# Weight chunks reloaded as two half chunks, with a semaphore and a key for each half

## The reference

```python
# block 1: gated causal convolution, D_MODEL 2048, D_INNER 4096, 4 taps
xi, gate = split(layernorm(x) @ w_in.T)
xc = depthwise_causal_conv(xi, conv_w) + conv_b
x  = x + (silu(xc) * D * silu(gate)) @ w_out.T
# block 2: 8 experts (I_MOE 1024), top 2 of them weighted, and a shared FFN (I_SH 4096)
t = layernorm(x)
combine = normalised top-2 of softmax(t @ w_gate)
routed  = sum_e combine[:, e] * ((silu(t @ G_e) * (t @ U_e)) @ w_down_e)
shared  = (silu(t @ G_s) * (t @ U_s)) @ w_sh_down
x = x + routed + shared
```

## Time and profile before

| | us |
|---|---|
| median of 2 runs | 7186.25 |
| those runs | 7082.07 and 7290.44 |
| the profiled execution, time | 6710.59 |
| its span, slowest core (0) | 6709.0 |
| its spans, all cores | 6646.2 to 6709.0 |

### The profile page before, as it was taken

How to read it: one execution, slowest core, us unless ns; L and a number is a source line. 1 busy time by engine, 2 the same in 40 slices (tenths; PEclk the granted TensorE clock), 3 DMA queues, 4 the chain that set the end, 5 groups by cost and what they waited for, 6 DMA issues and landing times.

```text
span 6709.0 us, 69985 instructions; the slowest of 8 cores (6646.2 to 6709.0 us)
## 1 busy us (share of the span) xinstructions
PE 5761.2 (86%) x26243; PEld 2537.3 (38%) x26768; DVE 1529.4 (23%) x3001; ACT 984.1 (15%) x1469; POOL 1.3 (0%) x10
## 2 busy tenths in 40 slices
PE   4777899999699877776776798999999898999998
PEld 2333344433344333332332343444444343444443
DVE  3333233322222222222111322011100322011100
ACT  1222122211112111111111112000000111000000
POOL 0000000000000000000000000000000000000000
PEclk9998999999899998898888899999999999999999
DMA  7997988877434499999999433444444333444444
GB/s 217 278 288 255 309 291 291 286 271 260 174 132 137 137 308 305 304 297 303 298 292 300 146 131 112 146 143 145 145 141 143 135 132 111 146 146 145 143 142 147
DMA packets 190480, 1380.81 MB, mean 206 GB/s; under 512 B 21955, under 2 KB 22211, under 8 KB 131395
## 3 DMA queue, kind: packets, MB, share of 16 engines
q1 hardware_dynamic: 184320, 1342.52, 61.1%
q10 hardware_dynamic: 5830, 33.78, 1.4%
HBM read 1158.08 MB, written 218.10 MB: 205 GB/s over the span
## 4 chain that ended last, share of the span: by engine, by line
PE 68%; DMA 21%; DVE 5%; issue 4%; ACT 2%; SPq 0%; DVEq 0%; ACTq 0%; another core or an unknown queue 0%
PE p L414 65%; DMA xt<-ws 19%; DVE wbuf L349 2%; PE p L603 2%; ACT wbuf L348 2%; DMA xt<-x 1%; PE pb L516 1%; PE pb L636 0%; DVE big L453 0%; DVE xlt L530 0%; DVE big L494 0%; SPq L365 0%; DVE xib L579 0%; DVE diag L593 0%; DMA crow<-cem 0%
## 5 line engine op out<-in xcount | busy, mean ns | idle before, releaser
L414 PE MATMUL p<-xlt,wbuf 128*128 128x512 bf16 x16038 | 3686.8, 385 | 322.3 <-ACT sgb L758 114.1
L414 PEld LDWEIGHTS p<-xlt,wbuf 128*128 128x128 bf16 x16384 | 1590.3, 99 | 2378.4 <-issue 596.0
L414 PE MATMUL p<-big,wbuf 128*128 128x512 bf16 x8024 | 1850.4, 385 | 137.8 <-PE p L414 54.2
L414 PEld LDWEIGHTS p<-big,wbuf 128*128 128x128 bf16 x8192 | 789.1, 99 | 1161.2 <-issue 307.1
L349 DVE CAST wbuf<-xt 128x3072 bf16<-128x3072 f32 x285 | 501.5, 1760 | 1425.5 <-DMA xt<-ws 942.2
L348 ACT CAST wbuf<-xt 128x3072 bf16<-128x3072 f32 x142 | 390.7, 2752 | 1864.8 <-DMA xt<-ws 1211.0
L758 ACT ACTIVATE sgb<-p 128x512 bf16<-128x512 f32 x384 | 224.5, 595 | 1621.1 <-PE p L414 1600.1
L762 DVE TENSOR_TENSOR ev<-sgb,p 128x512 bf16<-128x512 bf16 x256 | 175.5, 686 | 1076.8 <-PE p L414 860.2
L647 DVE TENSOR_TENSOR xt<-xt,pb 128x512 f32<-128x512 f32 x128 | 87.7, 686 | 1108.8 <-PE pb L636 1108.8
L774 DVE TENSOR_TENSOR big<-sgb,p 128x512 bf16<-128x512 bf16 x128 | 87.8, 686 | 636.7 <-PE p L414 536.0
L611 ACT ACTIVATE sgb<-p 128x512 bf16<-128x512 f32 x128 | 76.4, 597 | 842.2 <-PE p L414 765.2
(11 more groups left out here) (76 smaller groups left out, 669.9 us busy)
## 6 DMA issues: line engine op xcount, KB each, us to landing
xt<-ws SPq DMA_DIRECT2D x427, 1536.0 KB, 11.7
wbuf<-wsb SPq DMA_DIRECT2D x597, 768.0 KB, 4.3
wsb<-wbuf SPq DMA_DIRECT2D x256, 768.0 KB, 10.0
xt<-x ACTq DMA_DIRECT2D x4, 4096.0 KB, 27.0
out<-xt ACTq DMA_DIRECT2D x4, 4096.0 KB, 14.0
crow<-cem ACTq DMA_DIRECT2D x32, 1.0 KB, 4.3
ev<-wg ACTq DMA_DIRECT2D x1, 64.0 KB, 10.0
cw_s<-cw ACTq DMA_DIRECT2D x1, 64.0 KB, 15.0
```

The lines of the kernel that those rows point to most:

```text
L414: ins = t.matmul(psum_ap, tiles[i][0], rhs_list[i], start=(grp_start and is_first and j == 0), stop=(grp_stop and is_last and j == len(idx ...
```

## The change

A reloaded chunk comes in as two transfers of 384 KB, tiles 0 to 11 and 12 to 23, each with its own semaphore (`wh0` to `wh5`, two to a slot). The key of a chunk is split in two, `("wch", chunk, half)`. The first half's transfer waits for the readers of both halves of chunk b - 3; the second stands right behind it in SP's queue and waits for nothing. A cast writes both keys and a write-back reads both, so staged chunks are moved as before. `wtiles` gives the half with each tile, and `mm_group` cuts a group wherever chunk or half changes, in all four passes, for staged chunks too. `HCT = 12`.

```diff
@@ flush_wloads
-                sy_op("wh%d" % (b % NSLOT), ld,
-                      reads=[("wsb", b % NCH)], wars=[("wch", b - NSLOT)],
-                      writes_clean=[("wch", b)])
+                for h in range(2):
+                    def ld(s, b=b, slot=slot, h=h):
+                        return s.dma_start(
+                            wbuf[:, (slot * CT + h * HCT) * 128:
+                                 (slot * CT + (h + 1) * HCT) * 128],
+                            wsb_h[b % NCH][:, h * HCT * 128:(h + 1) * HCT * 128])
+                    sy_op("wh%d" % ((b % NSLOT) * 2 + h), ld,
+                          reads=[("wsb", b % NCH)],
+                          wars=([("wch", b - NSLOT, 0), ("wch", b - NSLOT, 1)]
+                                if h == 0 else []),
+                          writes_clean=[("wch", b, h)])
@@ emit_stage_cast
-                  writes=[("wch", b)], wars_extra=[("wch", b - NSLOT)])
+                  writes=[("wch", b, 0), ("wch", b, 1)],
+                  wars_extra=[("wch", b - NSLOT, 0), ("wch", b - NSLOT, 1)])
@@ on_first_claim (write-back)
-                sy_op("wb%d" % (a % NSLOT), wbk, reads=[("wch", a)],
+                sy_op("wb%d" % (a % NSLOT), wbk,
+                      reads=[("wch", a, 0), ("wch", a, 1)],
                       writes=[("wsb", a % NCH)])
@@ wtiles
-                                 ((t % (NSLOT * CT)) + 1) * 128], a))
+                                 ((t % (NSLOT * CT)) + 1) * 128], a,
+                            (t % CT) // HCT))
@@ mm_group
-                if tiles[i][1] != tiles[i - 1][1]:
+                if tiles[i][1:] != tiles[i - 1][1:]:
                     parts.append(cur)
...
-                chunks = sorted({tiles[i][1] for i in idxs})
-                ckeys = [("wch", c) for c in chunks]
+                ckeys = sorted({("wch", tiles[i][1], tiles[i][2])
+                                for i in idxs})
```

More of the change, by code:

```diff
@@ L275, in build_program @@
             if a >= NCH and not (a < 2 * NCH and (a % NCH) >= (NCH // 3 if NT > 1 else NCH)):
-                sname = "wh%d" % (a % NSLOT)
-                _whcnt[sname] = _whcnt.get(sname, 0) + 1
-                em.preset_write(("wch", a), sname, 16 * _whcnt[sname])
+                for h in range(2):
+                    sname = "wh%d" % ((a % NSLOT) * 2 + h)
+                    _whcnt[sname] = _whcnt.get(sname, 0) + 1
+                    em.preset_write(("wch", a, h), sname, 16 * _whcnt[sname])
         wg_stg = ev[:, 0:2 * KD * NE].bitcast(F32)
@@ L376, in on_first_claim @@
                 pend_loads.append(b)
+        HCT = CT // 2
         def wtiles(n):
```

## The result

The changed kernel is slower: its time is 1.0497 times that of the kernel before, with a 95% interval of 1.0425 to 1.057. The profiled execution takes 7019.26 us against 6710.59 us; the forecast on that level was 7,045.

A forecast was written before the change was run, and what follows sets the result against it. PE was taken to bound passes 2, 3, a third of pass 1 and most of pass 0: 215 + 36 + 68 + 15 = 334 us, giving 7,045 us on the profiled execution, 7,520 us on the median; range 7,000 to 7,680 us.

The forecast's parts named there:

- What bounds the kernel: Passes 2, 3 and the first third of pass 1 at PE's pace, staged chunks of pass 1 at DMA's; pass 0 changes over.
- The count of the new parts: All four passes: every chunk gets one more part in the middle of a group, 1,024 in all.
- The sign for the whole span: Profile after: PE waiting for PE listed 458 + about 1,000 times over the whole span.
- The price, 0.42 us: TensorE: each part waiting for the pe count of the part before it starts 0.42 us late.
- the prediction's estimate of 124 us: TensorE: by the skill page's difference alone, 760 waits x 0.16 us; the wait's way back is not in it.
- Two transfers for one at 0 us: SP queue: 597 more issues at 0.32 us, 191 us, all hidden; earlier first halves give nothing back.
- The half-counted 15 us of attn_up in pass 0: attn_up, 43 mixed chunks: new waits and cut halo groups, 43 x (0.42 + 0.28) = 30 us, half taken.
- the single figure of 7,520 us: Whole kernel: the 334 us sum added to the median of 7186.25 us of the kernel before.
- the price is the chunk edge's: Rival, 5%: 0.42 us comes from touching a newly written wbuf slot, so mid-chunk cuts are free; 7,186 us stays.
- the clock: Rival, 5%: new pauses bring the granted clock to 0.93 at PE's pace, 331 us more, 7,851 us on the median.
- hidden further: Rival, 12%: all of pass 0 stays at DMA's pace, only reloaded chunks pay; 251 us, 7,437 us on the median.
- late reloads: Rival, 3%: reloads were late in the two longer runs and half chunks shorten those waits; 7,186 us.

## Why the prediction was right

**What bounds the kernel.** Right. Passes 2 and 3 ran at PE's pace and took all of the new waits. Pass 1 took 44 us for the 36 forecast of its reloaded chunks; the 8 left for its staged chunks are within the spread of the cores. The stretch of after at 2700 us is as full of DMA as that of before at 2600. (Counted from 0, slice 10 has PE at 6 tenths, and slices 0 and 3 have DMA at 7, unlike the prediction's reading of the slices; nothing in its sum hangs on them.)

```profile
900.00:1000.00 100.00, 93.42 (x406) 38.33 (x413) 34.78 (x37) 23.68 (x19) 0.00 (x0) 1.00 0.74 264
2700.00:2800.00 100.00, 77.14 (x303) 29.77 (x306) 24.24 (x27) 16.70 (x14) 0.00 (x0) 0.90 0.97 299
...
6800.00:6900.00 100.00, 91.35 (x408) 37.97 (x417) 2.75 (x4) 2.35 (x4) 0.00 (x0) 1.00 0.42 134
```

**The count of the new parts.** Right: 401 listed in pass 2, forecast 405. The sign for the whole span, 458 + about 1,000, didn't come: 1,069 were listed, since the waits of the cuts in staged chunks stay under what the list shows.

**The price, 0.42 us, from shown length, visible idle time and true spacing.** Right where the added part has two waits: 212 us in passes 2 and 3 for a forecast of 215. Wrong for staged chunks, whose cut has only the own wait and costs 0.31 us. I took one price from chunk edges and did not ask which waits stood there. It shows in pass 0: 163 x 0.31 = 51 us where I had 68.

The Trainium skill (TensorE: Matmul & The Clock Gate, section Single matmul latency) gives 379 ns for one matmul; less the spacing of 216 ns measured here, its end past the next one's start is 0.16 us. The trace agrees: 379 ns is the median length that it shows too, though that end is modelled. The 0.31 us of a lone own wait are those 0.16 us and the 0.15 us of idle time; with the page's part alone the change would have cost the prediction's estimate of 124 us, and it cost 309.

**Two transfers for one at 0 us.** Right: PE's list of waits has none for a reload, and the transfers alone leave the time where it was, but for the 11 us of the third wait.

**The half-counted 15 us of attn_up in pass 0.** Pass 0 as a whole gained 62 us, and 51 are accounted for from 800 us on; the 11 left fit, but the cores of before differ by 30 us there, so this term isn't confirmed by itself.

**The whole.** 334 us forecast on the profiled execution, 309 measured from slowest core to slowest core, 318 between the means of the cores. The sum was right: pass 0 came out 21 us lower, pass 1 8 us higher. The added time was forecast well, the single figure of 7,520 us was not: it stands on a median of two executions of before, and the median of 11 of the changed kernel came out at 7,318. The 7,019 us lie just inside a range that had been drawn down to 7,000, 45 us under the sum, to take in this level. Of the rivals, "the price is the chunk edge's" fell with the cuts inside chunks, which cost 0.31 us without any transfer; "the clock" fell with the pauses after every sixth matmul at a granted clock of 1.00; "hidden further" fell with the 62 us of pass 0; "late reloads" found no support, as the half transfers alone gain nothing, but no trace of one of the longer executions of before was kept to look for such waits. At 88.8% busy, with a cut every 1.6 us, the granted clock was 1.00, the level of 2.4 GHz. The Trainium skill (TensorE: Matmul & The Clock Gate, section A second HAM failure mode: psum-queue depth-cycling) tells of a clock that swings with short idle times between groups of matmuls; this stretch shows no instance of it.

**What stays open.** In which part of the own wait's 0.15 us the time lies, the count's way or the wait's end, no run separates. The kernel before without the own wait and the changed kernel without it differ by less than the executions do, so whether halves are worth a microsecond in pass 0 isn't known.

## What to carry to other kernels

Look at what a dependency tracker makes of an engine's own writes: on TensorE a wait for the matmul just issued cost 0.31 us at 512 columns, and between parts accumulated into one bank, which nobody reads in between, it wasn't needed. Without it both kernels were 2 to 3% faster than the kernel before. Before splitting a transfer to have its first part earlier, find the wait that this shortens; here there was none, and the split's price was in the consumer, not in the queue. Where an own wait must stay, put it behind all others of the same instruction: that gave back 0.11 us a part in the changed kernel.

## What the runs showed of the hardware

Waits on PE aren't alike: one whose value was reached long ago cost nothing without an own wait (2,910 us for passes 2 and 3 with as many old waits, 2,909 with none) or ahead of it (3,158 us, 0.31 us a part), and 0.11 us behind it (3,247 us). The idle times of 0.15, 0.26 and 0.37 us for one, two and three waits, the own one first, make a ladder that can be read off a timeline. And idle time as shown is not the loss: with matmuls shown 0.38 us long and 0.216 us apart, each listed 0.26 us was 0.42 us lost.
